# Attention over 48 heads: the loop over groups of four heads written out on four engines

## What is computed

```python
x = x + attention(layernorm(x)) ; t = x + experts(layernorm(x))
# attention, for each of 4 images x 12 heads = 48 heads, n = 1024 tokens, hd = 16
bias = rel_h[:, :, :, :, None] + rel_w[:, :, :, None, :]        # from q and two position tables
attn = softmax(q * scale @ k.T + bias, axis=-1)                 # 1024 x 1024
out  = attn @ v
```

## Time and profile before

| | us |
|---|---|
| median of 3 runs (878.61 to 881.58) | 880.63 |
| the profiled execution, own time | 887.1 |
| its span | 884.8 |
| TensorE busy (matmul) | 785.4, 89% of the span |
| VectorE busy | 724.5, 82% |
| ScalarE busy | 608.8, 69% |
| GpSimd busy | 284.8, 32% |

### The profile page before, as it was taken

One profiled execution on the slowest core, in us unless ns is written; L12 is line 12 of the kernel. 1 busy time (PEld: TensorE's weight loads), 2 busy tenths in 40 slices (PEclk: granted clock), 3 DMA queues, 4 the chain that ended last, 5 costly groups with the idle time before them and its releaser, 6 DMA issues. The chain is left out here.

```text
span 884.8 us, 32156 instructions
## 1 busy us (share of the span) xinstructions
PE 785.4 (89%) x11946; PEld 487.2 (55%) x11946; DVE 724.5 (82%) x1022; ACT 608.8 (69%) x1139; POOL 284.8 (32%) x437
## 2 busy tenths in 40 slices
PE   3999938999999999999999999999988617999994
PEld 1768802444444444444444444444478617999994
DVE  6876767998999999999999999899347485888883
ACT  3675605888888888888888888888845603544442
POOL 5530000023343423303232233421015304666662
PEclk9999956999999999999999999999989657999998
DMA  6255973345555545444454545543044402222310
GB/s 175 72 144 176 365 225 101 101 126 135 137 145 139 134 128 135 125 120 129 135 137 132 140 135 145 150 125 84 4 179 133 166 0 75 81 82 83 97 57 8
DMA packets 69738, 109.71 MB, mean 124 GB/s; under 512 B 20139, under 2 KB 36681, under 8 KB 68146
## 3 DMA queue, kind: packets, MB, share of 16 engines
q1 hardware_dynamic: 59120, 75.49, 30.5%
q0 software_dynamic: 9248, 26.51, 10.6%
q10 hardware_dynamic: 1314, 6.95, 2.1%
HBM read 77.58 MB, written 33.19 MB: 125 GB/s over the span
## 5 line engine op out<-in xcount | busy, mean ns | idle before, releaser
L913 DVE TENSOR_REDUCE neg_max<-max_ps 128x1 f16<-128x1024 f32 x384 | 451.9, 1221 | 41.6 <-PE max_ps L762 33.9
L896 ACT ACTIVATE probs<-ring_ps 128x512 f32<-128x512 f32 x768 | 413.7, 596 | 68.7 <-PE ring_ps L796 60.0
L796 PE MATMUL ring_ps<-q_side,k_side 113*32 113x512 f16 x3072 | 241.1, 386 | 11.6 <-DMA q_side<-rel_split 8.3
L808 PE MATMUL out_ps<-probs,values 128*32 128x256 f32 x3072 | 200.4, 380 | 0.2 <-ACT probs L896 0.2
L762 PE MATMUL max_ps<-k_side,q_side 48*128 48x256 f16 x1536 | 137.5, 280 | 18.0 <-ACT ident L871 9.3
L808 PEld LDWEIGHTS out_ps<-probs,values 128*32 128x32 f32 x3072 | 92.7, 110 | 70.9 <-issue 1.0
L796 PEld LDWEIGHTS ring_ps<-q_side,k_side 113*32 113x32 f16 x3072 | 73.2, 94 | 96.8 <-ACT probs L896 38.7
L658 POOL COPY max_copies<-neg_max 128x32 f16<-128x32 f16 x48 | 10.1, 210 | 350.4 <-DVE neg_max L913 350.4
L762 PEld LDWEIGHTS max_ps<-k_side,q_side 48*128 48x128 f16 x1536 | 49.1, 95 | 121.9 <-issue 70.1
L1467 PE MATMUL hid_ps<-slot_t,w_top 128*118 128x128 f16 x312 | 69.0, 221 | 0.8 <-ACT slot_t L1513 0.8
L1468 PE MATMUL hid_ps<-slot_t,w_top 128*118 128x128 f16 x312 | 68.8, 221 | 0.0
(11 more groups left out here) (230 smaller groups left out, 1357.0 us busy)
## 6 DMA issues: line engine op xcount, KB each, us to landing
q_side<-rel_split SPq DMA_DIRECT2D x384, 64.0 KB, 2.3
q_side<-qk_split SPq DMA_DIRECT2D x192, 64.0 KB, 2.5
rel_split<-expert_weights ACTq DMA_DIRECT2D x6, 1024.0 KB, 4.9
rel_split<-expert_weights SPq DMA_DIRECT2D x6, 1024.0 KB, 6.1
q_side<-qk_split SPq DMA_DIRECT2D x48, 128.0 KB, 2.8
k_side<-qk_split SPq DMA_DIRECT2D x144, 32.0 KB, 1.8
token_rows<-tn_parts SPq DMA_DIRECT2D x8, 512.0 KB, 3.4
expert_weights<-in_w_t POOLq DMA_DIRECT2D x32, 117.2 KB, 3.0
```

Of the source, the lines that this page charges most:

```text
L796: last = nc.tensor.matmul(ring_ps[turn_of(k) % BANKS][at:at + COLS, :], k_side[slot(s)][:, tile * P + at:tile * P + at + COLS], queries, s ...
L808: last = nc.tensor.matmul(out_ps[quarter * 2 * HD:(quarter + 1) * 2 * HD, :], values[j][:, tile, :], probs[:, u % 2 * GROUP + 2 * i + quar ...
L896: nc.scalar.activation(probs[:, u % 2 * GROUP + i, :], ring_ps[turn_of(k) % BANKS][:], ACT.Exp).then_inc(exp_done, 1)
L913: nc.vector.tensor_reduce(neg_max[:, j % 2, t:t + 1], max_ps[t % 2][:], AX, ALU.max, negate=True).then_inc(tile_max, 1)
```

## The change

On TensorE, ScalarE, VectorE and SyncE the call of `steps` becomes a loop in Python over all 48 heads, so that each head's instructions stand in the program once for each head, with every number known when it is built. No wait, buffer, tile or order of work is changed. The `Step` objects have `known=True`, so that the conditions `before` and `after` are decided when the program is built; GpSimd's code is as it was. The expert stage still uses `steps`.

```diff
--- before.py
+++ after.py
@@ -612,6 +612,12 @@
 
             return s.group + (s.slot + ahead) // SLOTS
 
+        def every_head(step):
+
+
+            for n in range(BH):
+                step(Step(n, n // SLOTS, n % SLOTS, BH, True))
+
         block = ctx.enter_context(nc.Block())
 
         @block.sync
@@ -640,7 +646,7 @@
                 if s.after(3):
                     load_positions(sp, g, head(s, 3), slot(s, 3))
 
-            steps(sp, BH, SLOTS, step)
+            every_head(step)
 
         @block.gpsimd
         def _(pool):
@@ -861,7 +867,7 @@
                         bank_free(s, TURNED_AT)
                         turn_out(s.n - 1)
 
-            steps(pe, BH, SLOTS, step)
+            every_head(step)
             weighted_values(BH - 1, (BH - 1) % SLOTS, PAIR_TILES - 1)
             pe.wait_ge(exp_done, 2 * KT * BH)
             turn_out(BH - 1)
@@ -900,7 +906,7 @@
 
                             copy_max(s.n + 1, slot(s, 1), head(s, -1) + 1 if s.before(1) else None)
 
-            steps(act, BH, SLOTS, step)
+            every_head(step)
             copy_out(BH - 1, True)
 
         @block.vector
@@ -941,7 +947,7 @@
                     if u == 2 and s.before(1):
                         normalize(s.n - 1, head(s, -1), slot(s, -1), s.before(2))
 
-            steps(dve, BH, SLOTS, step)
+            every_head(step)
             normalize(BH - 1, HEADS - 1, B - 1, True)
```

## The result

The changed kernel takes 885.86 us (median of 20 runs, 881.07 to 893.09) and the kernel before 880.66 (20 runs, 877.24 to 886.89). The ratio is 1.0054, 95% interval 1.0029 to 1.0078: slower by 2.6 to 6.9 us. Single executions of one kernel lie several us apart, in the stages around the attention too, so that the profiled execution after has a span of 881.7 us, less than the 884.8 of before. What the change does is therefore read in the attention stage, from the first to the last `transpose_max` after the start, one a head.

A forecast was written before the change was run, and what follows sets the result against it. VectorE was taken to set the pace, 10.33 us a head, TensorE close behind and sometimes waiting for loads. Terms -2.4 - 0.3 - 2.1 + 4.0 + 6.3 = +5.5 us on 880.6 gave 886 us, range 876 to 893.

The forecast's parts named there:

- VectorE's register work and the branch: VectorE's loop: dropping a register instruction saves 0.06 us a head, -2.4 us; dropping the branch at each pass's end, -0.3 us.
- SyncE's register work: SyncE's load issue in the loop: without register instructions loads end earlier and late heads wait less, -2.1 us.
- the loads end about 0.3 us earlier: SyncE's queue: from `store_max` to the end of the last position load takes 4.26 us written out, for 4.57.
- the 7 late heads get up to 0.3 us each: Heads where TensorE waits for loads: each gains up to 0.3 us, -2.1 us, or nothing if DMA backlog sets the landing.
- q8 is TensorE's code, one packet for 264 instructions: DMA queue q8 carries TensorE's instructions; written out, 227 to 603 us needs 48 fetches that were not there.
- stays in its buffer: TensorE's loop: a pass of 4 heads, once fetched in the first pass, needs no further fetch; no size given.
- A fetch stalls SyncE's issue: SyncE's load issues: an issue seems to stand still until TensorE's code fetch is over, costing 1.3 to 1.4 us.
- (b): Fetch among position loads of usual heads: landing late beyond the cover, 0.2 us in 20 heads, +4.0 us, bounds 0 and 5.2.
- (c): Fetch in late heads, which have no cover: 6 heads at 1.05 us, +6.3 us, bounds 4.2 and 9.9.
- the fetch counts up to the landing: Late heads: a fetch anywhere up to the loads' landing costs time, 83% of the head, some 6 of 7 heads.
- In a late head there is no cover: Late heads: no spare time between landing and scores, so a fetch costs 1.05 us, with 0.3 us of backlog in the low bound.
- fetches hidden: Rival: stalls fall at product loads or within late heads' backlog, so fetches cost nothing; -4.8 us, 875.8 us, chance 0.18.

The follow-up runs named there:

- e4: Changed kernel with the loop put back on all engines but VectorE, which alone stays written out: 879.08 us, ratio 0.9976 to the kernel before.
- e8: Changed kernel with the loop put back on all engines but SyncE, which alone stays written out: 881.95 us, ratio 1.0001 to the kernel before.
- e1: Changed kernel with TensorE's loop over four heads put back, ScalarE, VectorE and SyncE still written out: 880.12 us, ratio 1.0001 to the kernel before.
- e11: Repeat, unchanged, of the changed kernel with only TensorE put back in its loop over four heads: 879.39 us, ratio 0.9963 to the kernel before.
- e2: Changed kernel with the loop put back on SyncE, ScalarE and VectorE, TensorE alone written out: 886.54 us, ratio 1.0078 to the kernel before.
- e5: Changed kernel with four of the eight position loads issued ahead of `store_max`: 871.97 us, ratio 0.9896 to the kernel before.
- e10: Changed kernel with work left out: split-weight stores gathered at head 5, later ones cut to one of 128 rows; 885.33 us, ratio 1.0036 to the kernel before.
- e7: Changed kernel with TensorE back in its four-head loop and four position loads issued ahead of `store_max`: 871.92 us, ratio 0.9878 to the kernel before.
- e9: Kernel before with work left out: split-weight stores gathered at head 5, later ones cut to one of 128 rows; 886.27 us, ratio 1.0054 to it.
- e6: Kernel before, all loops kept, with four of the eight position loads issued ahead of `store_max`: 877.60 us, ratio 0.9927 to it.
- e3: Changed kernel with TensorE in a loop of 8 heads a pass, the other three engines written out: 903.38 us, ratio 1.0256 to the kernel before.

## Why the prediction was right

The forecast was 886 with a range of 876 to 893, slower at 0.58; 885.86 was measured. The direction and the mechanism were right: TensorE's fetched code holds up SyncE's loads, and that costs more than VectorE gains. The sum hit partly because errors in its terms cancel.

- **VectorE's register work and the branch**, -2.4 and -0.3: right. The period fell from 10.33 to 10.28, with the unrounded starts 2.6 to 2.7 us over 46 intervals; e4 gives -3.5 in the stage, 0.4 of it in the heads across a pass's end.
- **SyncE's register work**, -2.1: wrong, e8 shows +0.4, nothing. Two steps failed. The first is "the loads end about 0.3 us earlier": by e8 the issues end 0.2 us earlier and the loads land 0.07 us earlier. The second is "the 7 late heads get up to 0.3 us each": the three kernels that have SyncE written out and no fetches (e1, e11, e8) lose 5.5 to 6.5 us in the late heads, the two that have it in its loop 5.3.
- **q8 is TensorE's code, one packet for 264 instructions**: right. From 225 to 605 us q8 has 1 or 2 packets in every kernel with TensorE's loop over 4 heads, 50 in the changed kernel and in e2, where TensorE alone is written out, 52 in e5 and 51 in e10. In the changed kernel the 50 from 227 to 603 us go with 6318 + 6320 instructions of TensorE, one for 253. That a pass of 4 heads "stays in its buffer" no run shows; they show the counts, 1 packet with passes of 4 heads and 56 with passes of 8.
- **A fetch stalls SyncE's issue**: right. 50 packets for the 48 worked out; 42 of 612 SyncE issues between 225 and 605 us took over 0.9 us (none of 616 before), the longest 1.99. All 42 overlap a packet on q8 and most end 0.36 us after it. TensorE's own stream shows no stop at a fetch in the changed kernel: its matmuls waited for loads alone, and no wait of a weight load that is put down to its own issue is over 0.4 us. e1 and e2 tie the loss to TensorE's code, e5 and e7 tie the price to the cover of the loads.
- **(b) usual heads**, +4.0 with bounds of 0 and 5.2: "others" went from 1.2 to 6.5, +5.3, and in e2 +4.0. Of the 5.3 us, 1.7 lie in the first eight intervals, nearly all of which have fetches in the kernel before too; from interval 9 on it is +3.7, which is what the term was for. So the size was right, but not what it was made of: 0.2 us in each of 20 heads. It is 11 heads that lost 0.1 to 0.7 us, and hardly anything in the rest. Without SyncE's 0.3 the cover is 0.84 and not 1.14, and the trace agrees: where the loads landed 7.5, 7.64 and 7.92 us after `store_max` (some 6.45 undisturbed), the head lost 0.24, 0.38 and 0.66 us, each time the delay less about 0.8.
- **(c) late heads**, +6.3 with a low bound of 4.2: wrong. They went from 5.3 to 6.1, and even the 0.8 isn't clear of the scatter, as e11 has 6.5 without a fetch. Two steps failed. The first, "the fetch counts up to the landing", made it 6 of 7 heads. All seven had a fetch there, but only in two (36 and 39) did it stretch a position load for long; in the others it came with the end of the last issue or after it, as the prediction had said that it might, at one and the same place. The second is "In a late head there is no cover": where the issue was stretched, its landing was hardly later. Head 36, the last position load and the scores that waited for it:

```profile
517.84 1.83 SPq L542 DMA_DIRECT2D q_side<-rel_split  x1
...
521.74 0.61 PE L802 MATMUL ring_ps<-q_side,k_side 113*32 113x512 f16 x8 [0.61 <-DMA q_side<-rel_split]
```

That load landed 2.0 us after its issue ended, where late heads have 3.2 to 3.5 in the mean in the kernels without fetches, and 8.05 us after `store_max`, where those have 7.9 to 8.04. Head 39 is the same with 2.0 and 8.06. The time for which a late landing waits in any case takes up the stretched issue. I had set 0.3 us for it. Two heads are few to show this by, and that the wait is for the backlog of the DMA engines rests on e9 and e10 (in e9 six of the late intervals fell from 4.4 to 1.5 us).

- **Together**, by the trace: -2.6 for 46 periods, +5.3, +0.8 and -0.5 for the interval 6 make +3.0, the stage's own difference. The forecast of +5.5 is 2.5 over it: (c) with SyncE's term was +4.2 and is +0.8, and the 1.7 us of the first eight intervals, for which there was no term, make up half of what is missing. TensorE's matmuls accordingly waited 6.4 us for loads and not the 12 that were named. The timed difference, 5.2 us with 2.6 to 6.9, holds both, so the close hit of the median is partly luck.
- **The rival "fetches hidden"** didn't come in the changed kernel; it is what e5 is, by another order of loads.

A fetch also delays loads that have been issued already. In the heads 28, 33, 38 and 43 of the changed kernel it began 0.6 to 0.9 us after the last position load's issue had ended, and that load landed 3.1 to 3.3 us after the start of its issue. In e1, e11 and e8, which have no fetch there, the same loads took 2.2 to 2.5. So the stretched issue is not the whole of what a fetch does to the loads.

What stays open: why head 16 is late without the store; and how a fetch holds up both an issue and loads under way, since the issue on SyncE's queue and the DMA engine that carries the code's packet weren't tried apart. With four loads moved (e6) the rest landed 1.7 us earlier in usual heads and 2.6 us earlier in the late ones (5.35 us after `store_max` for 7.98). That is more than the longest wait there, so these heads fell from 5.3 to 0.1 us; why they gained more than the usual ones isn't shown.

## What to carry to other kernels

Before a loop is written out, ask which engine's pace it sets and how much code is fetched then. Here the register work was worth 0.06 us of 10.33 a head on VectorE, which sets the period (e4, stage -3.5), and nothing on SyncE (e8, stage +0.4). TensorE's code, some 6350 matmuls and as many weight loads in 376 us, brought 50 packets on q8 written out, 56 in a loop of 8 heads and 1 in a loop of 4; the other three engines' brought 17 on q14. In straight code a fetch cost TensorE nothing here: its matmuls waited for loads alone, 6.4 us. It was paid through SyncE's loads, so look at how long before its use a load lands. Here the last one had a cover of 0.84 us in a usual head, and it was worth moving four of them into a wait of their queue, in either kernel: that alone took the ratio from 1 to 0.993 for the kernel before, and from 1.005 to 0.990 for the changed one.

## What I had not expected of the hardware

- A fetch of TensorE's code (q8, 16 KB, some 0.9 to 1.6 us) stretched SyncE's DMA issues from 0.42 to as much as 1.99 us, but not those of GpSimd in the attention: their median was 0.54 us with a fetch beside them (17 issues, 0.56 at most) and without. Loads already issued landed some 0.8 us later (3.1 to 3.3 us after the start of their issue for 2.2 to 2.5).
- A branch back over 8 heads cost 6.2 to 7.4 us a time, in a stretch with 56 packets on q8 (e3); at one back over 4 heads, in a stretch with no packet on it, the head takes 10.36 for 10.33 us.
- Written-out TensorE code showed no cost in TensorE's own time: heads stood at 10.27 to 10.28 us where no load was late, in the changed kernel with 50 packets as in e1 with 1.
